# A transformer block and a linear attention block on one core: style preparation from VectorE to ScalarE, and the last two exponent rounds joined

## The chip, the cores and the metric
The kernel runs on one core of one Trainium2 chip. The metric is device time in microseconds of one launch, the median of several runs. One profiled execution stands beside them; its span, from the first to the last instruction, is what the views of the trace show.

## The reference
The input x holds 16 sequences of 128 tokens with 128 features, fp32. A conditioned transformer block is followed by a conditioned linear attention block:

```python
# block 1 (16 heads of 8 dimensions)
mod = c @ ada_w.T + ada_b                     # shift, scale, gate, twice
h = rmsnorm(x) * (1 + sc) + sh
q, k, v = split(h @ qkv_w.T)
q, k = rope(rmsnorm(q)), rope(rmsnorm(k))
attn = softmax(q @ k.T / sqrt(8))
x = x + g_msa * (attn @ v @ proj_w.T + proj_b)
h2 = rmsnorm(x) * (1 + sc2) + sh2
x = x + g_mlp * ((silu(h2 @ w1.T) * (h2 @ w3.T)) @ w2.T)
# block 2
xn = layer_norm(x) * norm_g + norm_b
q, k, v = xn @ Wq + bq, xn @ Wk + bk, xn @ Wv + bv
y = softmax_d(q) @ (softmax_n(k).T @ v)
scale, shift = split(silu(emb) @ emb_W + emb_b)
h = layer_norm(y, sn_g, sn_b) * (1 + scale) + shift
out = x + gate * (silu(h) @ out_W + out_b)
```

## The kernel before
The program is written by hand engine by engine; each engine has one instruction stream, and semaphores tie them together. A prologue loads and transposes the weights. Then the main loop runs over t = 0 to 17 (LAST_A = B + 2). Its pass t works on several sequences at once: scores of sequence t + 2, exponent products of sequence t, weighted values of t, their transposition to tokens and division for t - 1, the output projection of t - 2, and the front (norm, modulation, queries, keys, values) of t + 6. From t = 14 on the feed-forward of the first pairs of sequences (units) starts inside the loop: b_first, b_input and b_rest. After the loop blocks_tensor, blocks_vector, blocks_scalar and blocks_gpsimd finish the feed-forward and run the second block.

Attention scores are computed twice. First TensorE makes queries times keys for all four groups of heads, and VectorE takes each row's negated maximum (rowmax, L1604) and writes it into the padded queries, whose keys hold a one at that place. Then TensorE makes keys times queries again with the maximum subtracted in the product, and ScalarE takes the exponent straight from PSUM (exp, L1302). Heads have 8 dimensions, padded to 16, so one product uses 32 rows of the array: a row group. round_(t, r) (L1870) issues the scores of sequence t + 2 on two row groups (L1886) and the exponent products of sequence t on the other two (L1895), for r = 0 and 1. Scores go to banks 0 and 1 (S_BANK), exponent products to banks 2 and 3 (E_BANK), in both rounds, so round 1 waits until ScalarE has read round 0's banks (s_p) and VectorE the scores' (s_max). For t = 14 and 15 there is no sequence t + 2 left, and both rounds hold exponent products only.

weighted_values(t, r) (L1975) multiplies values by the exponents of round r; ScalarE's summed(t) (L1371) copies the result, TensorE's token_major(t) and projection(t - 1) follow in the next pass. ScalarE's order in a pass is: exp(t, 0), from t = 15 on the tanh of hidden column 0, from t = 14 on b_input (L566), queries_and_max (L1328), exp(t, 1), attended (L1363), from t = 15 on the tanh of hidden columns 1 and 2 (L575), summed(t), spread_of(t - 2), and at t = 10 outw (L1473).

hidden(t, p, c) on TensorE (L863, L864) makes column block c of the feed-forward's hidden layer; the banks are GU_BANK = (0, 1, 4). At t = 15 b_first makes block 0 after projection and token_major, and b_rest makes blocks 1 and 2 between weighted_values(15, 0) and weighted_values(15, 1).

The preparation of block 2's parameters is spread over the loop. style() (L1564) on VectorE, issued at the end of t = 8, makes csilu (the silu of the condition, two operations of 128x16), nbb (norm_b in all columns, 128x128) and lin (the three weights times norm_g, 128x384). prepare_biases(part) (L1834) on TensorE multiplies biases with the weights in three parts, at t = 10, 11 and 12; prepare_centred (L1853, product at L1855) follows at t = 13. biases() at t = 13 and centred() at t = 14 on VectorE copy the results. In the profile, lines of the page are those of the kernel printed below; L846 to L992 are TensorE's products of the feed-forward and of block 2.

Of the kernel before, what the change touches and what calls it, by code (L numbers as in the profile page):

```python
# [32 lines left out]
B, T, D = 16, 128, 128  # L33
# [13 lines left out]
NC = 4  # L47
# [65 lines left out]
def dit_then_linear_attention(nc, x, cond, pos, norm1_w, qkv_w, q_norm_w, k_norm_w, proj_w, proj_b,  # L113
# [3 lines left out]
    with ctx:  # L117
# [104 lines left out]
        def two(name, *shape):  # L222
# [45 lines left out]
        GU_BANK, F_BANK, X_BANK = (0, 1, 4), (2, 3), 7  # L268
# [139 lines left out]
        A_SQUARE, A_QKV, A_MID, A_SIN, A_ADA, A_W1, A_W3, A_TANH, A_GB, A_DONE, A_ROWS, A_SQUARES, A_OUTW = (  # L408
            1, 2, 3, 4, 5, 6, 7, 8, 9, 11, 12, 20, 21)
        V_COND, V_ADA1, V_MS, V_MOD, V_QKW, V_ANG, V_MSMID, V_MODR, V_MODS, V_LIN, V_BIAS, V_DONE = (  # L410
            2, 3, 5, 8, 9, 18, 20, 22, 24, 28, 34, 35)
# [24 lines left out]
        def scored(b, r, i):  # L436

            if b < EARLY:
                return ((s_s0, s_s1), (h_s0, h_s1))[r][i], b + 1
            return (s_s0, s_s1)[i], ROUNDS * b + r - 1  # L440

# [396 lines left out]
        def blocks_tensor(e, start=None):  # L838
# [14 lines left out]
            def hidden(t, p, c):  # L853
                u = t + 1
                if is_unit(u):
                    if c == 0:
                        e.wait_ge(b_hT, u + 1)
                        if at(u, 0):
                            e.wait_ge(s_max, NC * B)
                            e.wait_ge(s_kq, B)  # L860
                            e.wait_ge(pv_v, V_DONE)
                    wait(e, b_ff, FC * (u - 1) + c + 1)
# [48 lines left out]
            def c_step(t):  # L911
# [25 lines left out]
                if is_part(u):  # L937
                    hold_clock(t, 2 if t < C_UNITS + 3 else 4)
                    e.wait_ge(d_hs, u + 1)
                    if u == 0:  # L940
                        e.wait_ge(pv_a, A_OUTW)
# [309 lines left out]
        def _(a):  # L1251
# [44 lines left out]
            def exp(t, r, i):  # L1296
# [5 lines left out]
                q.activation(probs[2 * r + i][:, :, :, :].rearrange("p f a t -> p (f a t)"), bank[E_BANK[i]][:, :],  # L1302
# [144 lines left out]
            for t in range(LAST_A):  # L1447
# [23 lines left out]
                if t == B - 6:  # L1471
                    a.wait_ge(ld_rest, N_REST)
                    q.activation(outw[:, :], outw_n[:, :], ACT.Copy, scale=0.5).then_inc(pv_a, 1)  # L1473
            blocks_scalar(a, 2)
# [4 lines left out]
        def _(v):  # L1479
# [84 lines left out]
            def style():  # L1564

                v.wait_ge(pv_a, A_TANH)
                did(q.scalar_tensor_tensor(csilu[:, :], ctanh[:, :], 1.0, condT[:, :], ALU.add, ALU.mult))
                did(q.tensor_scalar(csilu[:, :], csilu[:, :], 0.5, None, ALU.mult))
                count(q.tensor_scalar(nbb[:, :], par[:, R_NB:R_NB + 1].to_broadcast([128, 128]), 1.0, None, ALU.mult))
                v.wait_ge(ld_rest, N_REST)  # L1570
                count(q.tensor_scalar(lin[:, :, :], lin_n[:, :, :], par[:, R_NG:R_NG + 1], None, ALU.mult))
                assert n == V_LIN

            def biases():
# [3 lines left out]
                did(q.tensor_tensor(embr[:, :, :], bank[W_BANK][:, 3 * D:3 * D + 2 * B].rearrange("p (c b) -> p c b", b=B),  # L1578
                                    par[:, R_EB:R_EB + 2].unsqueeze(2).to_broadcast([128, 2, B]), ALU.add))
# [501 lines left out]
```

## Time and profile before
| what | value |
|---|---|
| median of 3 runs | 207.35 us (207.1 to 209.03) |
| the profiled execution, its own time | 207.43 us |
| its span | 205.4 us |
| TensorE (PE) busy | 180.9 us, 88% of the span |
| VectorE (DVE) busy | 166.1 us, 81% |
| GpSimd (POOL) busy | 141.3 us, 69% |
| ScalarE (ACT) busy | 129.4 us, 63% |
| DMA | 8.30 MB, mean 40 GB/s |

Busy shares are means over the whole span; the stretch that the change touches is from 77 to 127 us, and a small edit near 36 us. PEld is TensorE's weight load, which overlaps its products. An fp32 product counts as two records of each kind, so the 8 products of a round of exponents show as 16 records. In a timeline "[0.35 <-PE bank L1895]" means that the engine had been idle for 0.35 us, and that the instruction named ended the wait.

### The profile page before, as it was taken

To read this page: it belongs to the slowest core of one execution; us is meant where nothing else is said; L and a number is where in the kernel's file an instruction comes from. 1 tells how busy PE (TensorE), PEld (TensorE's weight loads), DVE (VectorE), ACT (ScalarE), POOL (GpSimd) and SP (SyncE) were. 2 spreads that over 40 slices of the span, in tenths; PEclk is the share of its full clock that TensorE was granted. 3 is DMA by queue.
4 is the path that set the end of the run, shared out by engine and by line. 5 is a ranking of instruction groups with operands and counts; after the bars stand their busy time and mean duration, and the time that the engine had idled before them with its cause. 6 is when DMAs were issued, how large, how long until landed. Compare 5 with 4: busy or idle time off the path is not lost.

```text
span 205.4 us, 6100 instructions
## 1 busy us (share of the span) xinstructions
PE 180.9 (88%) x2039; PEld 142.3 (69%) x2039; DVE 166.1 (81%) x498; ACT 129.4 (63%) x377; POOL 141.3 (69%) x333
## 2 busy tenths in 40 slices
PE   2598887997999999799999998899998899999963
PEld 2345565786687777677676777799997677888642
DVE  6699898896989999997776534668889799999882
ACT  1367798776867777576546763454442468999741
POOL 8889798998989797958810682434542847668651
PEclk9999999999999999999999999999999999999999
DMA  5955006800000000000000000000000000010111
GB/s 93 289 137 207 0 10 254 359 6 0 3 3 2 5 5 0 3 0 5 3 3 0 5 0 3 0 0 5 2 0 2 0 3 0 0 30 28 51 51 51
DMA packets 10428, 8.30 MB, mean 40 GB/s; under 512 B 3106, under 2 KB 9887, under 8 KB 9887
## 3 DMA queue, kind: packets, MB, share of 16 engines
q1 hardware_dynamic: 7006, 7.25, 10.3%
q10 hardware_dynamic: 3392, 0.68, 1.7%
q8 instruction: 16, 0.26, 0.6%
q14 instruction: 14, 0.11, 0.2%
HBM read 6.86 MB, written 1.07 MB: 39 GB/s over the span
## 4 chain that ended last, share of the span: by engine, by line
PE 40%; DVE 17%; issue 8%; POOL 5%; ACT 4%; POOLq 0%; ACTq 0%; DVEq 0%
PE bank L1895 5%; DVE qkpad L1604 5%; PE bank L875 5%; PE bank L1886 5%; PE bank L863 5%; PE bank L864 4%; PE bank L1975 4%; ACT probs L1302 2%; PE bank L908 2%; POOL rstd L515 2%; PE bank L1907 1%; PE bank L1920 1%; PE bank L992 1%; PE bank L1949 1%; PE bank L972 1%
## 5 line engine op out<-in xcount | busy, mean ns | idle before, releaser
L1604 DVE TENSOR_REDUCE qkpad<-bank 128x4 f32<-128x512 f32 x64 | 41.0, 684 | 10.1 <-PE bank L1886 9.2
L1302 ACT ACTIVATE probs<-bank 128x512 f32<-128x512 f32 x64 | 34.7, 594 | 22.6 <-PE bank L1895 22.5
L1895 PE MATMUL bank<-qTm,kBD 32*128 32x128 f32 x512 | 37.1, 283 | 0.1
L1886 PE MATMUL bank<-kBD,qTs 32*128 32x256 f32 x224 | 32.0, 399 | 4.4 <-DVE qkpad L1604 3.4
L1895 PEld LDWEIGHTS bank<-qTm,kBD 32*128 32x128 f32 x512 | 31.0, 186 | 0.9 <-issue 0.6
L1886 PEld LDWEIGHTS bank<-kBD,qTs 32*128 32x128 f32 x224 | 19.7, 184 | 10.3 <-DVE qkpad L1604 6.3
L575 ACT ACTIVATE th<-bank 128x256 f32<-128x256 f32 x24 | 9.2, 384 | 19.4 <-PE bank L864 16.0
L1975 PE MATMUL bank<-probs,vpad 128*32 128x128 f32 x512 | 18.6, 277 | 2.0 <-ACT probs L1302 2.0
L1975 PEld LDWEIGHTS bank<-probs,vpad 128*32 128x32 f32 x512 | 12.6, 109 | 8.4 <-ACT probs L1302 7.3
L1130 POOL TENSOR_TENSOR partner<-qk,rope 128x96 f32<-128x96 f32 x32 | 14.4, 471 | 2.0 <-ACT qk L1344 2.0
L1949 PE MATMUL bank<-qkvT,hT 128*128 128x384 f32 x32 | 15.3, 571 | 0.5 <-ACT hT L1319 0.5
L1920 PE MATMUL bank<-ident,qkpad 128*128 128x128 f32 x96 | 14.2, 277 | 1.4 <-POOL qkpad L1192 1.1
L674 DVE SCALAR_TENSOR_TENSOR yg<-th,bank 128x256 f32<-128x256 f32 x24 | 10.1, 419 | 5.8 <-ACT th L575 5.8
L505 POOL TENSOR_TENSOR x<-fg,x 128x256 f32<-128x256 f32 x6 | 4.4, 730 | 14.9 <-DVE fg L691 14.9
L863 PE MATMUL bank<-hT,w1T 128*128 128x256 f32 x48 | 14.4, 382 | 0.0
L864 PE MATMUL bank<-hT,w3T 128*128 128x256 f32 x48 | 14.3, 379 | 0.0
L875 PE MATMUL bank<-w2T,ff 128*128 128x128 f32 x96 | 13.2, 275 | 0.0
L1920 PEld LDWEIGHTS bank<-ident,qkpad 128*128 128x128 f32 x96 | 10.8, 141 | 3.1 <-POOL qkpad L1192 1.7
L875 PEld LDWEIGHTS bank<-w2T,ff 128*128 128x128 f32 x96 | 12.4, 191 | 0.4
L515 POOL TENSOR_TENSOR rstd<-var,minus_half 128x2 f32<-128x2 f32 (+1 forms) x17 | 11.7, 687 | 1.4
L1141 POOL TENSOR_TENSOR rot<-qk,rope 128x256 f32<-128x256 f32 x16 | 11.7, 729 | 0.0
L1192 POOL TENSOR_TENSOR qkpad<-rot,ny 128x256 f32<-128x256 f32 x15 | 9.7, 647 | 2.2 <-DVE ny L1701 0.4
(253 smaller groups left out, 521.4 us busy)
## 6 DMA issues: line engine op xcount, KB each, us to landing
gate<-in_cond_dram SPq DMA_DIRECT2D x1, 1024.0 KB, 4.7
x<-gate_rows SPq DMA_DIRECT2D x1, 1024.0 KB, 4.3
y<-gate_rows SPq DMA_DIRECT2D x1, 1024.0 KB, 6.4
res<-gate_rows SPq DMA_DIRECT2D x1, 1024.0 KB, 9.8
out_dram<-res SPq DMA_DIRECT2D x7, 128.0 KB, 1.8
xin<-in_x_dram ACTq DMA_DIRECT2D x2, 256.0 KB, 5.4
xin<-in_x_dram SPq DMA_DIRECT2D x1, 512.0 KB, 5.7
ada_n<-in_L_cond_ada_w_dram SPq DMA_DIRECT2D x1, 256.0 KB, 6.2
```

Source lines behind the costliest of these rows:

```text
L515: q.tensor_tensor(rstd[:, rows], var[:, rows], minus_half[:, 0:rows.stop - rows.start], ALU.pow).then_inc(made, 1)
L863: q.matmul(bank[GU_BANK[c]][:, 0:UNIT * T], w1T[:, c * 128:c * 128 + 128], flat(hT2[1 - p]), start=True, stop=True)
L864: q.matmul(bank[GU_BANK[c]][:, UNIT * T:], w3T[:, c * 128:c * 128 + 128], flat(hT2[1 - p]), start=True, stop=True).then_inc(b_gu, 1)
L875: last = q.matmul(bank[F_BANK[j]][:, 0:D], ff[c][:, j * T:(j + 1) * T], w2T[:, c, :], start=c == 0, stop=c == FC - 1)
L1130: last = q.tensor_tensor(heads(partner[b % 2][:, :, :])[:, :, :, k::2], heads(qk[b % NQK][:, :, :])[:, :, :, 1 - k:ROPE:2], table(b, 1)[:, ...
L1302: q.activation(probs[2 * r + i][:, :, :, :].rearrange("p f a t -> p (f a t)"), bank[E_BANK[i]][:, :], ACT.Exp, scale=SCALE).then_inc(s_p, 1)
L1604: q.tensor_reduce(out_, score_bank(b, r, i)[:, :].rearrange("p (f a t) -> p f a t", f=2, a=2), X_AXIS, ALU.max, negate=True).then_inc(s_ma ...
L1886: last = q.matmul(bank[S_BANK[i]][:, f * 2 * T:(f + 1) * 2 * T], qTs[b % 2][rows, f, :], kBD[b % NKB][rows, f, :, :].rearrange("p a t -> p ...
L1895: last = q.matmul(bank[E_BANK[i]][:, (2 * f + k) * T:(2 * f + k + 1) * T], kBD[t % NKB][rows, f, k, :], qTm[t % 2][rows, f, :], start=True ...
L1920: last = q.transpose(dst[:, at_ + f * T:at_ + (f + 1) * T], qkpad[b % NKB][:, s, 8 * f:8 * f + 8, :].rearrange("p h d -> p (h d)"), ident[ ...
L1949: q.matmul(front_bank(b)[:, 128:512], hT[b % 2][:, :], qkvT[:, :], start=True, stop=True).then_inc(s_qkv, 1)
L1975: last = q.matmul(bank[O_BANK][32 * c:32 * c + 32, r * T:(r + 1) * T], vpad[b % NVP][:, col:col + VSTEP], probs[2 * r + i][:, f, k, :], st ...
```

## The change
style() keeps only the sum and product for csilu and is issued at t = 0; the factor 0.5 goes into embr. nbb and lin are made by ScalarE at the end of t = 10, behind outw. prepare_biases runs at t = 11, 12 and 13 and waits for ScalarE's two results (A_STYLE) in place of VectorE's. For t = 14 and 15 a new function exponents(t) issues all 16 exponent products of the sequence over four row groups, in four banks: those of r = 0 in banks 2 and 3, those of r = 1 in banks 0 and 1 (exp_bank); round_ isn't called there. It waits for all maxima (s_max). The hidden blocks go to banks 4, 0 and 1 in this order; block 0 of the first unit no longer waits for the maxima, blocks 1 and 2 wait for all exponents (s_p). weighted_values(t, 1) comes directly behind weighted_values(t, 0), ahead of b_rest at t = 15.

```diff
--- before.py
+++ after.py
@@ -265,7 +265,7 @@
 
         bank = [ctx.enter_context(nc.psum_tensor(f"bank{i}", [128, 512], F32)) for i in range(8)]
         S_BANK, E_BANK, T_BANK, P_BANK, O_BANK, W_BANK = (0, 1), (2, 3), 4, 5, 6, 7
-        GU_BANK, F_BANK, X_BANK = (0, 1, 4), (2, 3), 7
+        GU_BANK, F_BANK, X_BANK = (4, 0, 1), (2, 3), 7
         XC_BANK, QV_BANK, K_BANK, KT_BANK, CTX_BANK, QT_BANK, Y_BANK, XD_BANK, OUT_BANK = 7, 5, 6, 0, 1, 4, 2, 3, 0
 
 
@@ -405,10 +405,10 @@
         N_CONSTS = 10
         N_ROPE, N_ROPE_V = 8, 4
         P_COND, P_ADA1, P_MOD, P_QKV, P_ADA, P_MODS, P_PAR, P_W1, P_W3, P_W2, P_ROWS, P_BIAS, P_LIN = range(1, 14)
-        A_SQUARE, A_QKV, A_MID, A_SIN, A_ADA, A_W1, A_W3, A_TANH, A_GB, A_DONE, A_ROWS, A_SQUARES, A_OUTW = (
-            1, 2, 3, 4, 5, 6, 7, 8, 9, 11, 12, 20, 21)
-        V_COND, V_ADA1, V_MS, V_MOD, V_QKW, V_ANG, V_MSMID, V_MODR, V_MODS, V_LIN, V_BIAS, V_DONE = (
-            2, 3, 5, 8, 9, 18, 20, 22, 24, 28, 34, 35)
+        A_SQUARE, A_QKV, A_MID, A_SIN, A_ADA, A_W1, A_W3, A_TANH, A_GB, A_DONE, A_ROWS, A_SQUARES, A_STYLE = (
+            1, 2, 3, 4, 5, 6, 7, 8, 9, 11, 12, 20, 23)
+        V_COND, V_ADA1, V_MS, V_MOD, V_QKW, V_ANG, V_MSMID, V_MODR, V_MODS, V_CSILU, V_BIAS, V_DONE = (
+            2, 3, 5, 8, 9, 18, 20, 22, 24, 25, 31, 32)
 
         block = ctx.enter_context(nc.Block())
 
@@ -438,6 +438,10 @@
             if b < EARLY:
                 return ((s_s0, s_s1), (h_s0, h_s1))[r][i], b + 1
             return (s_s0, s_s1)[i], ROUNDS * b + r - 1
+
+        def exp_bank(b, r, i):
+
+            return bank[(S_BANK if r == 1 and b + 2 >= B else E_BANK)[i]]
 
         def front_bank(b):
 
@@ -856,9 +860,10 @@
                     if c == 0:
                         e.wait_ge(b_hT, u + 1)
                         if at(u, 0):
-                            e.wait_ge(s_max, NC * B)
                             e.wait_ge(s_kq, B)
                             e.wait_ge(pv_v, V_DONE)
+                    if c > 0 and at(u, 0):
+                        e.wait_ge(s_p, NC * B)
                     wait(e, b_ff, FC * (u - 1) + c + 1)
                     q.matmul(bank[GU_BANK[c]][:, 0:UNIT * T], w1T[:, c * 128:c * 128 + 128], flat(hT2[1 - p]), start=True, stop=True)
                     q.matmul(bank[GU_BANK[c]][:, UNIT * T:], w3T[:, c * 128:c * 128 + 128], flat(hT2[1 - p]), start=True,
@@ -938,7 +943,7 @@
                     hold_clock(t, 2 if t < C_UNITS + 3 else 4)
                     e.wait_ge(d_hs, u + 1)
                     if u == 0:
-                        e.wait_ge(pv_a, A_OUTW)
+                        e.wait_ge(pv_a, A_STYLE)
                     e.wait_ge(c_kxT, min(u + 4, C_UNITS))
                     for j in range(c_size(u)):
                         dst = bank[OUT_BANK][:, j * D:(j + 1) * D]
@@ -1299,7 +1304,7 @@
                     return
                 a.wait_ge((s_e0, s_e1)[i], ROUNDS * t + r + 1)
                 wait(a, s_o, ROUNDS * (t - 1) + r + 1)
-                q.activation(probs[2 * r + i][:, :, :, :].rearrange("p f a t -> p (f a t)"), bank[E_BANK[i]][:, :],
+                q.activation(probs[2 * r + i][:, :, :, :].rearrange("p f a t -> p (f a t)"), exp_bank(t, r, i)[:, :],
                              ACT.Exp, scale=SCALE).then_inc(s_p, 1)
 
             def spread_of(b):
@@ -1471,6 +1476,9 @@
                 if t == B - 6:
                     a.wait_ge(ld_rest, N_REST)
                     q.activation(outw[:, :], outw_n[:, :], ACT.Copy, scale=0.5).then_inc(pv_a, 1)
+                    q.activation(nbb[:, :], ident[:, :], ACT.Identity, bias=par[:, R_NB:R_NB + 1], scale=0.0).then_inc(pv_a, 1)
+                    q.activation(lin[:, :, :].rearrange("p c f -> p (c f)"), lin_n[:, :, :].rearrange("p c f -> p (c f)"), ACT.Identity,
+                                 scale=par[:, R_NG:R_NG + 1]).then_inc(pv_a, 1)
             blocks_scalar(a, 2)
 
 
@@ -1564,19 +1572,15 @@
             def style():
 
                 v.wait_ge(pv_a, A_TANH)
-                did(q.scalar_tensor_tensor(csilu[:, :], ctanh[:, :], 1.0, condT[:, :], ALU.add, ALU.mult))
-                did(q.tensor_scalar(csilu[:, :], csilu[:, :], 0.5, None, ALU.mult))
-                count(q.tensor_scalar(nbb[:, :], par[:, R_NB:R_NB + 1].to_broadcast([128, 128]), 1.0, None, ALU.mult))
-                v.wait_ge(ld_rest, N_REST)
-                count(q.tensor_scalar(lin[:, :, :], lin_n[:, :, :], par[:, R_NG:R_NG + 1], None, ALU.mult))
-                assert n == V_LIN
+                count(q.scalar_tensor_tensor(csilu[:, :], ctanh[:, :], 1.0, condT[:, :], ALU.add, ALU.mult))
+                assert n == V_CSILU
 
             def biases():
                 v.wait_ge(pt, P_BIAS)
                 count(q.tensor_copy(bias_qvo[:, :], bank[W_BANK][:, 0:3 * D]))
                 count(q.tensor_tensor(bias_k[:, :], bank[W_BANK][:, 3 * D + 2 * B:3 * D + 2 * B + 1], par[:, R_BK:R_BK + 1], ALU.add))
-                did(q.tensor_tensor(embr[:, :, :], bank[W_BANK][:, 3 * D:3 * D + 2 * B].rearrange("p (c b) -> p c b", b=B),
-                                    par[:, R_EB:R_EB + 2].unsqueeze(2).to_broadcast([128, 2, B]), ALU.add))
+                did(q.scalar_tensor_tensor(embr[:, :, :], bank[W_BANK][:, 3 * D:3 * D + 2 * B].rearrange("p (c b) -> p c b", b=B), 0.5,
+                                           par[:, R_EB:R_EB + 2].unsqueeze(2).to_broadcast([128, 2, B]), ALU.mult, ALU.add))
                 count(q.tensor_scalar(mods[:, :, A3], embr[:, 0, :], 1.0, par[:, R_SG:R_SG + 1], ALU.add, ALU.mult))
                 did(q.tensor_scalar(mods[:, :, S3], embr[:, 0, :], 1.0, par[:, R_SB:R_SB + 1], ALU.add, ALU.mult))
                 did(q.tensor_tensor(mods[:, :, S3], mods[:, :, S3], embr[:, 1, :], ALU.add))
@@ -1759,7 +1763,6 @@
                     b_rest(t - B)
                 if t == 0:
                     gates()
-                if t == B - 8:
                     style()
                 if t == B - 3:
                     biases()
@@ -1834,7 +1837,8 @@
             def prepare_biases(part):
 
                 if part == 0:
-                    e.wait_ge(pv_v, V_LIN)
+                    e.wait_ge(pv_a, A_STYLE)
+                    e.wait_ge(pv_v, V_CSILU)
                     e.wait_ge(s_v, B)
                     e.wait_ge(ld_rest, N_REST)
                     e.wait_ge(consts, 5)
@@ -1893,6 +1897,22 @@
                                 row = 32 * (2 * r + i)
                                 rows = slice(row, row + 32)
                                 last = q.matmul(bank[E_BANK[i]][:, (2 * f + k) * T:(2 * f + k + 1) * T], kBD[t % NKB][rows, f, k, :],
+                                                qTm[t % 2][rows, f, :], start=True, stop=True)
+                                if f == 1 and k == 1:
+                                    last.then_inc((s_e0, s_e1)[i], 1)
+
+            def exponents(t):
+
+                e.wait_ge(s_qTm, t + 1)
+                e.wait_ge(s_max, NC * B)
+                e.wait_ge(s_p, NC * t)
+                for f in range(2):
+                    for k in range(2):
+                        for r in range(2):
+                            for i in range(2):
+                                row = 32 * (2 * r + i)
+                                rows = slice(row, row + 32)
+                                last = q.matmul(exp_bank(t, r, i)[:, (2 * f + k) * T:(2 * f + k + 1) * T], kBD[t % NKB][rows, f, k, :],
                                                 qTm[t % 2][rows, f, :], start=True, stop=True)
                                 if f == 1 and k == 1:
                                     last.then_inc((s_e0, s_e1)[i], 1)
@@ -2020,7 +2040,10 @@
             modulation_rows()
             b_first, b_input, b_rest = blocks_tensor(e)
             for t in range(LAST_A):
-                round_(t, 0)
+                if t < B - 2:
+                    round_(t, 0)
+                elif t < B:
+                    exponents(t)
                 projection(t - 2)
                 token_major(t - 1)
                 if t == B - 1:
@@ -2033,20 +2056,21 @@
                 queries_and_max(t + 1)
                 queries_and_keys(t + 3)
                 input_turned(t + 6)
-                if B - 6 <= t < B - 3:
-                    prepare_biases(t - (B - 6))
+                if B - 5 <= t < B - 2:
+                    prepare_biases(t - (B - 5))
                 if t == B - 3:
                     prepare_centred()
                 if t == B - 2:
                     b_input(t - B, t % 2)
-                round_(t, 1)
+                if t < B - 2:
+                    round_(t, 1)
                 queries_keys_values(t + 6)
                 if t < B:
                     attended(t - 1)
                 weighted_values(t, 0)
+                weighted_values(t, 1)
                 if t == B - 1:
                     b_rest(t - B, t % 2)
-                weighted_values(t, 1)
                 if t >= B:
                     b_input(t - B, t % 2)
                     b_rest(t - B, t % 2)
```

## Rows read from the trace of the kernel before

**Rows 1.** The page, chain that ended last: shares of the span by engine.
```profile
PE 40%; DVE 17%; issue 8%; POOL 5%; ACT 4%; POOLq 0%; ACTq 0%; DVEq 0%
```
**Rows 2.** Busy time by stretch (from:to length, busy us (count) per engine, granted clock, DMA).
```profile
65.22:71.24 6.02, 5.63 (x98) 4.45 (x94) 5.92 (x15) 4.37 (x13) 4.93 (x15) 1.00 0.02 4
71.24:76.86 5.62, 5.62 (x98) 4.48 (x94) 4.97 (x13) 4.42 (x14) 5.36 (x12) 1.00 0.02 4
...
82.60:89.46 6.86, 5.64 (x99) 4.46 (x95) 6.78 (x17) 4.40 (x14) 4.98 (x10) 1.00 0.01 2
89.46:95.28 5.82, 5.41 (x97) 4.25 (x94) 5.63 (x14) 3.48 (x11) 4.50 (x14) 1.00 0.01 4
...
113.27:118.54 5.27, 4.84 (x77) 3.74 (x73) 2.52 (x11) 4.10 (x11) 3.90 (x7) 1.00 0.02 5
118.54:126.40 7.86, 7.31 (x88) 5.70 (x84) 3.03 (x10) 5.35 (x16) 5.56 (x12) 1.00 0.01 2
126.40:155.00 28.60, 28.07 (x178) 25.48 (x179) 22.07 (x75) 12.43 (x38) 12.13 (x22) 1.00 0.00 1
```
**Rows 3.** Timeline of VectorE, step 9 (start us, us, engine, line, operation, out<-in).
```profile
83.03 0.39 DVE L1567 SCALAR_TENSOR_TENSOR csilu<-ctanh,condT 128x16 f32<-128x16 f32 x1
83.46 0.65 DVE L1568 TENSOR_SCALAR csilu<-csilu 128x16 f32<-128x16 f32 x1
84.14 0.43 DVE L1569 TENSOR_SCALAR nbb<-par 128x128 f32<-128x128 f32 x1
84.50 0.64 DVE L1571 TENSOR_SCALAR lin<-lin_n,par 128x384 f32<-128x384 f32 x1
85.06 1.28 DVE L1604 TENSOR_REDUCE qkpad<-bank 128x4 f32<-128x512 f32 x2
```
**Rows 4.** Timeline of TensorE, step 9, its second round.
```profile
86.39 0.48 PE L1886 MATMUL bank<-kBD,qTs 32*128 32x256 f32 x2 [1.22 <-DVE qkpad L1604]
```
**Rows 5.** Timeline of VectorE after t = 0.
```profile
36.52 0.69 DVE L1604 TENSOR_REDUCE qkpad<-bank 128x4 f32<-128x512 f32 x1 [0.80 <-PE bank L1886]
```
**Rows 6.** Timeline of ScalarE, first exponent of step 11.
```profile
96.60 0.60 ACT L1302 ACTIVATE probs<-bank 128x512 f32<-128x512 f32 x1 [0.32 <-PE bank L1895]
```
**Rows 7.** Chain that ended last, steps 11 and 12 (start us, us, what).
```profile
97.09 0.66 PE bank L1920 x6
...
103.56 0.41 PE bank L1845 x2
...
104.75 0.32 PE bank L1886
```
**Rows 8.** Timeline of ScalarE, step 14.
```profile
115.60 0.81 ACT L566 ACTIVATE hT<-bank,mods 128x128 f32<-128x128 f32 x2
116.31 0.38 ACT L1328 ACTIVATE qTm<-bank 128x256 f32<-128x256 f32 x1
116.83 1.08 ACT L1302 ACTIVATE probs<-bank 128x512 f32<-128x512 f32 x2
```
**Rows 9.** Timeline of ScalarE, step 15.
```profile
122.55 1.08 ACT L1302 ACTIVATE probs<-bank 128x512 f32<-128x512 f32 x2 [0.22 <-PE bank L1895]
...
125.31 0.38 ACT L575 ACTIVATE th<-bank 128x256 f32<-128x256 f32 x1 [0.48 <-PE bank L864]
125.91 0.38 ACT L1371 ACTIVATE oT<-bank 128x256 f32<-128x256 f32 x1 [0.22 <-PE bank L1975]
```
**Rows 10.** Chain that ended last, step 15.
```profile
123.35 0.63 PE bank L863 x2
...
125.27 0.57 PE bank L1975 x16
```
**Rows 11.** Timeline of TensorE: early scores, weighted values, a round of exponents alone.
```profile
21.13 1.15 PE L1865 MATMUL bank<-kBD,qTs 32*128 32x256 f32 x16 [0.56 <-DVE qTs L1641]
...
75.85 1.08 PE L1975 MATMUL bank<-probs,vpad 128*32 128x128 f32 x32
...
113.27 1.16 PE L1895 MATMUL bank<-qTm,kBD 32*128 32x128 f32 x16
```

## The prediction
> **What bounds the kernel now.** I read the chain of work that ended last first, then the table of busy time by stretch, then the timelines of single engines. In the chain TensorE leads with 40% and VectorE follows with 17% [rows 1]. So neither is the bound everywhere, and each edit must be priced in its own step. I call step t the pass of the main loop that starts with TensorE's round_(t, 0); the table's stretches are steps 6, 7, 9, 10, 14, 15 and what follows up to 155 us [rows 2]. The granted clock is 1.00, the upper level of 2.4 GHz, in all of them, so no clock effect enters.
>
> In steps 6 and 7 TensorE is busy 5.63 and 5.62 us, but the steps last 6.02 and 5.62. Even steps, where VectorE also seeds the square roots of the head norms, are set by VectorE (5.92 of 6.02); odd steps by TensorE. Step 9 is odd and has TensorE's usual 5.64 busy, yet it lasts 6.86, with VectorE busy 6.78 [rows 2]. In steps 14 and 15 TensorE is busy 4.84 of 5.27 and 7.31 of 7.86; these hold the rounds that the change joins. ScalarE's exponents stand between TensorE's products there.
>
> **The style work leaves VectorE (step 9).** style() is issued at the end of t = 8 and runs in step 9: 0.39 + 0.65 + 0.43 + 0.64 = 2.11 us, and the row maxima behind it start at 85.06 [rows 3]. TensorE's second round waits for them 1.22 us [rows 4]. With the block gone step 9 becomes like step 7: 6.86 - 5.62 = 1.24 us won. The two ways of pricing it agree within 0.02. It can't be 2.11, as the products behind the maxima end only later.
> The one operation that stays on VectorE (csilu, 0.39) now runs at t = 0, where VectorE stands idle 0.80 us before its next maxima [rows 5]. Its input is ready before the loop, so it costs nothing; without that cover it would cost 0.39. Folding the factor 0.5 into embr changes one small operation for another of about its size, off the path.
>
> **ScalarE takes nbb and lin (end of t = 10).** Before shows no such activation. nbb (128x128) I price at the 0.40 of one of the two 128x128 modulations (0.81 for both) [rows 8]. lin (128x384) lies between the 128x256 copy, 0.38 [rows 9], and the 128x512 exponent, 0.60 [rows 6]; it is nearer the upper in elements and has a pointer scale besides, so 0.55. Together at most 1.0, some 0.75 after overlap of neighbours. ScalarE had 0.32 idle there before its exponents at 96.60 [rows 6], so these start about 0.4 late, and end 1.1 later at 98.1. TensorE's transposes end at 97.75, and the bias product that now follows them (0.41) fills it till 98.2 [rows 7]. Cost: 0 to 0.1, I take 0.05. If that cover went, it would be the 0.4.
> "ScalarE: Activation LUTs" of the Trainium skill ("Rules for kernel authors") speaks against this move: simple multiplies and adds belong on VectorE, which is faster per element. VectorE's 0.64 and 0.43 [rows 3] against the two prices above don't bear it out; by the rule ScalarE's start would slip past TensorE's cover, and the sum would be up to 0.4 higher.
>
> **The bias products move one step later on TensorE.** Part 2 lasts 104.75 - 103.56 = 1.19, and its first product, which streams about as much as part 0 and part 1 do each, 0.41 [rows 7]. Part 0 leaves step 10; in step 11 it takes the place of part 1, no change; part 1 takes the place of part 2 in step 12, and part 2 enters step 13.
> - Step 10: TensorE is ready 0.41 sooner; that is the most that can be won. At worst the step becomes like step 6, 6.02 against its 5.82 [rows 2]: +0.2. VectorE is busy 5.63 of 5.82 there and lets little through, so I take half the gain, -0.2.
> - Step 12: 1.19 - 0.41 = 0.78 won; the chain runs through part 2 without a break, and nothing else ends later than part 1 would.
> - Step 13: the chain also runs through the product before the second round, so all of 1.19 is added. VectorE reads these products at the end of the step, later than they then come.
> Steps 10 to 13 and ScalarE's 0.05: -0.2 - 0.78 + 1.19 + 0.05 = +0.26.
>
> **The joined rounds (steps 14, 15).** A round of exponents alone has 16 records on two row groups and takes 1.16. The early scores have 16 records on all four row groups, of twice the columns, thus the array work of a joined round, in 1.15; the weighted values put 32 records through four column groups in 1.08 [rows 11]. Before has no case of 32 records over four row groups. Lower bound 1.1: the groups run side by side and issue is no limit. Upper end 2.3: two rounds in a row. Two rows of the three stand near the lower one, so I take 1.2, thus 0.05 late per step.
> "TensorE: Matmul & The Clock Gate" of the Trainium skill ("Back-to-back issue gap") has 81 ns per sustained pair of load and product at 128 columns. By it a joined round takes 2.6 and the sum is about 2.8 higher; the weighted values' 34 ns a pair disagree for tiled products.
> What a joined round frees is a second round of 1.1 on TensorE. What takes its place is ScalarE's fixed order:
> - Step 14: exponents, two modulations, the copy qTm, exponents. qTm starts at 116.31 and, 0.38 long with neighbours overlapping by 0.1, would let exponents start at 116.6; before they started at 116.83 [rows 8]. Won 0.24, less 0.05. All of TensorE's other time is given back waiting for the last exponent.
> - Step 15: exponents started at 122.55 and ended at 123.63, after 0.22 idle; with the 0.1 by which neighbours overlap they come 0.3 sooner, 123.33 [rows 9]. But before, TensorE did the hidden products of columns 1 and 2 meanwhile (123.35 to 125.27, 1.92 [rows 10]), and the last weighted values (0.57) after. These products now write the banks that the last exponents read, and stand behind the weighted values. So: exponents end 123.33; weighted values till 124.0; hidden products till 125.9; tanh of column 2 starts 125.95 (before 125.31); the copy of the sums follows at 126.25 (before 125.91). It is 0.34 later, and TensorE's next projection with it. With 0.05 for the round: +0.39.
> The wait for s_max in exponents(14) costs nothing, since the maxima of the last sequence end before the weighted values of step 13 do. Behind the new wait for s_p on TensorE stand the two hidden products, and behind them tanh, the gate on VectorE and the copy of the sums: that is the 0.39. The bank permutation changes no duration. No DMA is issued, moved or passed by any edit. From 126.4 to 155 TensorE is busy 28.07 of 28.60 us [rows 2] with work that doesn't change, so whatever shift stands at 126.4 reaches the end.
> Steps 14 and 15: -0.19 + 0.39 = +0.20.
>
> **Sum.** -1.24 + 0.26 + 0.20 = -0.78 us. The profiled execution took 207.43 (span 205.4), 0.08 above the median 207.35. 207.4 - 0.8 = 206.6.
>
> **Rivals.**
> A. VectorE is late again in step 10 and gives back part of step 9: the even pattern of 6.02 [rows 2] in place of my 5.62 costs 0.4, 207.0. For it: VectorE is busy 5.63 of 5.82. Against: VectorE carries the same seeds in step 10 before the change too, and the step still takes 5.82. Chance 0.15.
> B. TensorE alone binds steps 14 and 15, and both removed rounds count in full: 2 x 1.16 in place of +0.20, 204.1. Against it: before the last exponents ScalarE is idle 0.22 only [rows 9], so it can't come 1.16 sooner. Chance 0.06.
> C, on the other side. The 32 pairs don't overlap beyond what two row groups show: 1.16 / 16 = 72 ns each, 2.3 us for a joined round. Then the first exponent of steps 14 and 15 starts 1.1 later, 2.2 in all less the 0.1 counted: 208.7, slower than before. It decides from where a joined round takes about 1.55 us (0.4 more in each step). Against it: the early scores and the weighted values [rows 11]. Chance 0.08. The figure of the Trainium skill's clock gate page, above, would make it slower still.
> D. The hidden products behind the last weighted values delay the whole gate: all 1.92 shows instead of 0.34, 208.1 at most. Against: the copy of the sums waits only for tanh of column 2. Chance 0.06.
> My forecast has the other 0.65.
>
> **Numbers.** 1% of 207.35 is 2.07, about what a measurement of this kernel can tell from no change. The range runs from the forecast's own lower edge (step 10 at -0.4, joined rounds at 1.1, ScalarE's activations free: 206.3, and 0.7 for step lengths that differ by 0.4 within one pattern: 205.6) to 207.9, near D's full price; it leaves out B and C, and a little beside, 0.2. Faster by over 1% needs 205.28 or less: B and a rest, 0.07. Slower by over 1% needs 209.42: C with more, 0.03. Within 1%: 0.90.
>
> **What would show it.** Right: step 9 at 5.6 and no wait for maxima in it; step 12 0.8 shorter and step 13 1.2 longer; 32 records of exponents in about 1.2; TensorE waiting for exponents over 1 us in steps 14 and 15; projection of sequence 14 starting 8.2 after step 15's start, not 7.86. Wrong: joined rounds over 1.5 us (C), step 15 under 7.5 us (B), step 10 at 6 us (A).

## The result and the profile after

The changed kernel takes 206.48 us, the median of 16 runs (206.18 to 207.55); the kernel before, beside it, 207.37 (207.01 to 209.03). The ratio is 0.995, with a 95% interval of 0.9933 to 0.9966. That is 0.9 us less; the forecast was 206.6, 0.8 less.

The profiled execution of after took 207.28 us with a span of 205.6, longer than the span of before (205.4). It is not a typical one: late in it TensorE's granted clock fell to the lower level, 1.2 GHz (0.74 on average in the last row here, 0.50 from 199.65 to 202.50), which costs 1.1 us, as the last section works out. So the steps are compared one by one, in stretches where the granted clock is 1.00. The table of busy time by stretch of after, for steps 9 to 15, for what follows up to the same work as at 155 us in before, and for the end:

```profile
core 0: us, PE busy (x) PEld busy (x) DVE busy (x) ACT busy (x) POOL busy (x), PEclk, DMA share, GB/s
82.53:88.15 5.62, 5.62 (x99) 4.48 (x95) 4.94 (x13) 4.42 (x14) 4.87 (x10) 1.00 0.01 3
88.15:93.66 5.51, 5.04 (x95) 4.00 (x91) 5.41 (x14) 3.46 (x10) 4.35 (x13) 1.00 0.02 4
93.66:99.54 5.88, 5.48 (x97) 4.28 (x93) 4.83 (x11) 4.17 (x12) 5.37 (x12) 1.00 0.02 3
99.54:105.37 5.83, 5.37 (x98) 4.16 (x94) 4.37 (x11) 3.29 (x9) 2.34 (x5) 1.00 0.00 0
105.37:112.24 6.87, 6.46 (x101) 4.80 (x97) 3.62 (x9) 3.29 (x9) 0.00 (x0) 1.00 0.01 2
112.24:117.27 5.03, 3.70 (x77) 2.79 (x74) 2.14 (x11) 3.98 (x11) 3.75 (x6) 1.00 0.02 5
117.27:125.46 8.19, 6.15 (x88) 4.72 (x84) 2.74 (x9) 5.13 (x16) 5.69 (x13) 1.00 0.00 0
...
125.46:154.06 28.60, 28.07 (x178) 25.48 (x179) 22.34 (x76) 12.43 (x38) 12.13 (x22) 1.00 0.01 2
199.00:205.60 6.60, 3.27 (x15) 2.25 (x15) 1.39 (x5) 0.77 (x2) 1.24 (x3) 0.74 0.13 40
```

The same table of before has steps 9, 10, 14 and 15 in [rows 2]; steps 11, 12 and 13 are:

```profile
95.28:101.10 5.82, 5.36 (x97) 4.15 (x94) 4.49 (x10) 3.49 (x10) 5.44 (x11) 1.00 0.02 3
101.10:107.67 6.57, 6.16 (x103) 5.02 (x99) 4.27 (x10) 3.29 (x9) 2.12 (x5) 1.00 0.01 2
107.67:113.27 5.60, 5.19 (x93) 3.81 (x89) 3.62 (x9) 3.29 (x9) 0.00 (x0) 1.00 0.00 0
```

Step lengths in us, measured and forecast:

| | step 9 | 10 | 11 | 12 | 13 | 14 | 15 | sum |
|---|---|---|---|---|---|---|---|---|
| before | 6.86 | 5.82 | 5.82 | 6.57 | 5.60 | 5.27 | 7.86 | 43.80 |
| after | 5.62 | 5.51 | 5.88 | 5.83 | 6.87 | 5.03 | 8.19 | 42.93 |
| difference | -1.24 | -0.31 | +0.06 | -0.74 | +1.27 | -0.24 | +0.33 | -0.87 |
| forecast | -1.24 | -0.2 | +0.05 | -0.78 | +1.19 | -0.19 | +0.39 | -0.78 |

The 28.60 us behind step 15 are 28.60 in both, to the hundredth, with 28.07 of TensorE's work. What stands at step 15's end does reach the end. It comes at 125.46 in place of 126.40, 0.94 sooner: 0.87 by these seven steps, and 0.07 that was already won at the start of step 9 (82.53 against 82.60).

In steps 14 and 15 TensorE has 1.14 and 1.16 us less to do than before (3.70 against 4.84, 6.15 against 7.31), a whole round each. The steps change by -0.24 and +0.33.

TensorE's timeline of after in steps 14 and 15 (start us, us, engine, line, operation, out<-in; in brackets the idle time before and what ended it):

```profile
112.24 1.17 PE L1915 MATMUL bank<-qTm,kBD 32*128 32x128 f32 x32
...
115.81 0.30 PE L2005 MATMUL bank<-ident,o 128*128 128x128 f32 x1 [1.32 <-ACT qTm L1333]
...
117.27 1.17 PE L1915 MATMUL bank<-qTm,kBD 32*128 32x128 f32 x32
...
122.09 0.65 PE L1995 MATMUL bank<-probs,vpad 128*32 128x128 f32 x16 [1.25 <-ACT probs L1307]
...
124.07 0.59 PE L869 MATMUL bank<-hT,w3T 128*128 128x256 f32 x2
125.46 0.46 PE L1927 MATMUL bank<-projT,oT 128*128 128x128 f32 x2 [0.80 <-issue]
```

The 32 records of a joined round take 1.17 us, 37 ns each; 16 records on two row groups take 1.16 [rows 11]. "TensorE: Matmul & The Clock Gate" of the Trainium skill ("Back-to-back issue gap") has 81 ns a pair; this trace does not agree for 32-row tiles. What was won shows as idle time: 1.32 before the transposes of step 14, 1.25 before the last weighted values.

ScalarE's timeline of after, step 15, shows why nothing comes of it there:

```profile
120.95 1.09 ACT L1307 ACTIVATE probs<-bank 128x512 f32<-128x512 f32 x2
...
123.84 0.39 ACT L579 ACTIVATE th<-bank 128x256 f32<-128x256 f32 x1 [1.63 <-PE bank L869]
124.70 0.38 ACT L579 ACTIVATE th<-bank 128x256 f32<-128x256 f32 x1 [0.48 <-PE bank L869]
124.98 0.38 ACT L1376 ACTIVATE oT<-bank 128x256 f32<-128x256 f32 x1
```

The copy of the sums (L1376) needs only the weighted values, which end at 122.7. It stands behind two tanh in ScalarE's fixed order, and these wait for the hidden products. TensorE's projection at 125.46 comes right behind the copy, which ends at 125.36; that it waits for the copy is tested below (sum_first), as the profile names only "issue" there.

### The profile page after: what moved, and what is told of

It is laid out like the page before. It is cut to its first block, busy times and chain, and to the rows that moved or that the text cites. A ratio compares the mean times of both kernels' runs of the same rounds, so it can differ in the third digit from the quotient of the medians.

```text
span 205.6 us, 6098 instructions
## 1 busy us (share of the span) xinstructions
PE 180.2 (88%) x2039; PEld 141.5 (69%) x2039; DVE 164.2 (80%) x495; ACT 129.8 (63%) x379; POOL 141.0 (69%) x333
## 3 DMA queue, kind: packets, MB, share of 16 engines
HBM read 6.86 MB, written 1.07 MB: 39 GB/s over the span
## 4 chain that ended last, share of the span: by engine, by line
PE 45%; DVE 14%; issue 8%; ACT 6%; POOL 3%; POOLq 0%; ACTq 0%; DVEq 0%
PE bank L1890 5%; PE bank L880 5%; PE bank L868 5%; PE bank L869 4%; PE bank L1995 4%; DVE qkpad L1608 4%; PE bank L1899 4%; PE bank L997 2%; ACT probs L1307 2%; PE bank L913 2%; PE bank L1940 2%; PE bank L1927 2%; PE bank L1969 2%; PE bank L1915 1%; PE bank L977 1%
## 5 line engine op out<-in xcount | busy, mean ns | idle before, releaser
L1899 PE MATMUL bank<-qTm,kBD 32*128 32x128 f32 x448 | 32.5, 283 | 0.0
L1899 PEld LDWEIGHTS bank<-qTm,kBD 32*128 32x128 f32 x448 | 27.1, 186 | 0.0
```

Source lines behind the costliest of these rows:

```text
L1899: last = q.matmul(bank[E_BANK[i]][:, (2 * f + k) * T:(2 * f + k + 1) * T], kBD[t % NKB][rows, f, k, :], qTm[t % 2][rows, f, :], start=True ...
```

## The experiments

All ratios are to the kernel before, measured beside each; its median was 207.11 for the first four experiments and 207.23 for the other four.

**One part each.** only_style is after with rounds, banks and order of before:

```
-        GU_BANK, F_BANK, X_BANK = (4, 0, 1), (2, 3), 7
+        GU_BANK, F_BANK, X_BANK = (0, 1, 4), (2, 3), 7
...
-                if t < B - 2:
-                    round_(t, 0)
-                elif t < B:
-                    exponents(t)
+                round_(t, 0)
...
-                if t < B - 2:
-                    round_(t, 1)
+                round_(t, 1)
...
                 weighted_values(t, 0)
-                weighted_values(t, 1)
                 if t == B - 1:
                     b_rest(t - B, t % 2)
+                weighted_values(t, 1)
```

> The style preparation and the bias products are moved as in the change, the exponent rounds and the hidden banks stay as before. Theory (the gain is the gap that the style work left in step 9, and the joined rounds cancel): steps 9 to 13 sum to -1.24 - 0.31 + 0.06 - 0.75 + 1.28 = -0.96 against before by the profile after, plus 0.1 measured ahead of step 8, so 206.4, ratio 0.995. Rival (the joined rounds bring part of the gain): this kernel gets at most half of the 0.89, 206.9.

Measured: 206.16 us, ratio 0.9958 (0.9936 to 0.9979). That is 0.95 us less. The rival, at most half of the change's 0.89, needs a ratio of 0.9979 or more, which is the very edge of the interval; the next experiment decides. only_rounds is the opposite, before with the joined rounds and all that goes with them:

> The joined exponent rounds, the hidden banks and the order of the weighted values alone, on the kernel before. Theory: step 14 is 0.24 shorter and step 15 0.33 longer, 207.4 to 207.5, ratio 1.0005. Rival (each removed round of 1.1 us on TensorE counts): 205.2, ratio 0.989.

Measured: 207.10 us, ratio 1.0004 (0.9985 to 1.0022). TensorE's timeline of only_rounds, the joined rounds and the projection of step 16:

```profile
113.41 1.17 PE L1916 MATMUL bank<-qTm,kBD 32*128 32x128 f32 x32
...
118.44 1.17 PE L1916 MATMUL bank<-qTm,kBD 32*128 32x128 f32 x32
...
126.63 0.46 PE L1928 MATMUL bank<-projT,oT 128*128 128x128 f32 x2 [0.80 <-issue]
```

118.44 - 113.41 = 5.03 and 126.63 - 118.44 = 8.19 are the step lengths of after. So the rounds come to -0.24 + 0.33 = +0.09 us, and a gain of two whole rounds (2.3 us, a ratio of 0.989) lies outside the interval. All that the change wins, it wins by the style work.

**Only the first round joined.** join14 joins for the sequence before the last and leaves the last as before, its hidden banks, waits and order of products too (the excerpt shows the rounds alone):

```
-                if t < B - 2:
-                    round_(t, 0)
-                elif t < B:
-                    exponents(t)
+                if t == B - 2:
+                    exponents(t)
+                else:
+                    round_(t, 0)
...
-                if t < B - 2:
+                if t != B - 2:
                     round_(t, 1)
```

> The changed kernel, but only sequence 14 has the joined round; sequence 15 has its two rounds, its banks and the hidden products between the weighted values, as before. Theory (the join costs in step 15 and gains in step 14): 0.33 less than the changed kernel, 206.15, ratio 0.994, and step 15 lasts 7.86 again instead of 8.19. Rival (the two joins are worth the same, or both nothing): as the changed kernel, 206.5.

Measured: 206.05 us, ratio 0.9941 (0.9921 to 0.9962). In its trace the projection stands at 125.36, with 0.55 idle before it in place of 0.80, 12.88 after step 14's start; in after that is 5.03 + 8.19 = 13.22. So -0.34 us, the price of the second joined round together with the order of products that it brings, found from the other side. The ratios alone, 0.9941 and 0.995, could not show it.

**The copy of the sums first.** sum_first lets ScalarE issue it ahead of the tanh, once:

```
+                if t == B - 1:
+                    summed(t)
                 if t >= B - 1:
                     b_rest(t - B)
                 if t >= B:
                     attended(t - 1)
-                summed(t)
+                if t != B - 1:
+                    summed(t)
```

> The changed kernel with one move on ScalarE at t = 15: the copy of the sums (summed) comes ahead of the tanh of hidden columns 1 and 2 instead of behind them. Theory (in step 15 TensorE's wait of 0.80 us before the projection of sequence 14 is only ScalarE's order): TensorE goes on from the hidden products to the projection at once, step 15 lasts 7.4 instead of 8.19, total 205.7, ratio 0.992. Rival (the wait is needed by something else, such as the gate products on VectorE, and comes back within step 16): 206.5 as the changed kernel, with the step after 0.8 longer.

Measured: 205.19 us, ratio 0.9912 (0.9883 to 0.9941). ScalarE's timeline of sum_first, the copy, which now waits only for the weighted values:

```profile
122.67 0.39 ACT L1376 ACTIVATE oT<-bank 128x256 f32<-128x256 f32 x1 [0.60 <-PE bank L1998]
```

Its TensorE timeline, the last hidden product and the projection, with no idle time between:

```profile
123.94 0.59 PE L869 MATMUL bank<-hT,w3T 128*128 128x256 f32 x2
124.37 0.39 PE L1930 MATMUL bank<-projT,oT 128*128 128x128 f32 x2
```

And its table by stretch, step 15 and the 32 matmul records behind it:

```profile
117.14:124.37 7.23, 5.99 (x88) 4.87 (x85) 1.81 (x7) 4.75 (x13) 5.66 (x13) 1.00 0.00 0
124.37:129.76 5.39, 4.86 (x32) 4.18 (x30) 4.38 (x15) 2.74 (x10) 1.59 (x3) 1.00 0.02 3
```

The 0.80 before the projection is gone, step 15 lasts 7.23 in place of 8.19, and the next stretch doesn't give it back (5.39; from 125.46 to 130.93, 5.47, in after). So ScalarE's order had held 0.96 us of step 15. Against before's 7.86 that is 0.63 won in step 15. How much of it is the joined round's, and how much would come from the new order of the products and of the copy with two separate rounds, is not shown: no run has that order with two rounds. The order alone could at most fill TensorE's wait before the projection, 0.55 without the join (join14).

**Place or engine.** late_dve gives nbb and lin back to VectorE, but at the end of t = 10; csilu stays at t = 0:

```
                 if t == B - 6:
                     a.wait_ge(ld_rest, N_REST)
                     q.activation(outw[:, :], outw_n[:, :], ACT.Copy, scale=0.5).then_inc(pv_a, 1)
-                    q.activation(nbb[:, :], ident[:, :], ...).then_inc(pv_a, 1)
-                    q.activation(lin[:, :, :]..., lin_n[:, :, :]..., ...).then_inc(pv_a, 1)
...
                     style()
+                if t == B - 6:
+                    style_rest()
```

> The changed kernel with nbb and lin back on VectorE, but at the end of t = 10 (csilu stays at t = 0) instead of on ScalarE there. Theory (the gain came from the place, since VectorE has an idle gap of over 1 us before the maxima of step 11 that holds 0.43 + 0.64 us): as the changed kernel, ratio 0.995, step 11 still 5.8 to 5.9. Rival (VectorE can't take this work anywhere in the loop, the engine matters): the maxima of step 11 come about 1 us late, as they did in step 9, ratio 0.999, step 11 at 6.8.

Measured: 206.11 us, ratio 0.9944 (0.9922 to 0.9966). VectorE's timeline of late_dve at that place:

```profile
93.71 0.21 DVE L1578 TENSOR_SCALAR nbb<-par 128x128 f32<-128x128 f32 x1
93.84 0.78 DVE L1579 TENSOR_SCALAR lin<-lin_n,par 128x384 f32<-128x384 f32 x1
```

ScalarE's timeline of after at the same place:

```profile
94.57 0.39 ACT L1479 ACTIVATE nbb<-ident,par 128x128 f32<-128x128 f32 x1
94.86 0.60 ACT L1480 ACTIVATE lin<-lin_n,par 128x384 f32<-128x384 f32 x1
```

VectorE takes 0.21 + 0.78, ScalarE 0.39 + 0.60: the same sum. late_dve's step 11, from TensorE's scores at 93.58 to those at 99.40, lasts 5.82, as in before; in after it lasts 5.88. So for these two operations the engine is worth 0.06, and the gain of step 9 didn't need ScalarE. VectorE's own work is 4.94 of 5.62 in step 9 of after, which leaves 0.68 for style's 2.11; in step 11 it is 4.83 of 5.88, which leaves 1.05 for these 0.99. The other 1.04 of the 2.11 were the two operations for csilu, one of which is gone and one at t = 0 in late_dve too; what nbb and lin alone would cost in step 9 no run shows. "ScalarE: Activation LUTs" of the Trainium skill ("Rules for kernel authors") puts multiplies and adds on VectorE, with a factor that it gives for bf16. These operations are fp32, and the traces show no clear winner: at 384 columns ScalarE took 0.60 and VectorE 0.78 here and 0.64 in before, at 128 columns ScalarE 0.39 and VectorE 0.21 here and 0.43 in before [rows 3].

**The centring product.** In after it runs in step 13, where TensorE is busy 6.46 of 6.87; in step 14 TensorE waits 1.32. centre14 moves it there:

```
-                if t == B - 3:
-                    prepare_centred()
                 if t == B - 2:
                     b_input(t - B, t % 2)
+                    prepare_centred()
```

> The changed kernel with the centring product (0.65 us on TensorE) moved from before the second round of step 13 to step 14 behind the transposes of the feed-forward's input, where TensorE waits 1.32 us for ScalarE. Theory (bias and centring products ahead of the second round of step 13 stand in full on the path, and step 14 is bound by ScalarE): 0.65 less than the changed kernel, 205.6 to 205.8, ratio 0.992; step 13 at 6.2, step 14 still 5.03. Rival (step 13 is bound by the maxima, or step 14 by TensorE): as the changed kernel, ratio 0.995.

Measured: 205.50 us, ratio 0.9924 (0.9897 to 0.9951). TensorE's timeline of centre14, from the projection in step 13:

```profile
106.59 0.49 PE L1927 MATMUL bank<-projT,oT 128*128 128x128 f32 x2
...
111.62 1.18 PE L1915 MATMUL bank<-qTm,kBD 32*128 32x128 f32 x32
...
113.70 0.81 PE L1859 MATMUL bank<-lin,centre 128*128 128x384 f32 x2
115.19 0.30 PE L2005 MATMUL bank<-ident,o 128*128 128x128 f32 x1 [0.67 <-ACT qTm L1333]
```

Projection to joined round is 5.03 (after: 112.24 - 106.47 = 5.77), so -0.74. Step 14 still lasts 5.03: the product of 0.81 took 0.65 of the wait, which falls from 1.32 to 0.67.

**Everything together.** combo has the edits of sum_first, centre14 and late_dve. It also moves parts 0 and 1 of the bias products, and the four products of the condition, from before the second round to between the two halves of the weighted values, where TensorE waits about 0.4 us for exponents. Part 2's other products stay before the second round of step 13:

```
-                if B - 5 <= t < B - 2:
-                    prepare_biases(t - (B - 5))
                 if t == B - 3:
-                    prepare_centred()
+                    prepare_biases(2)
...
                 weighted_values(t, 0)
+                if t == B - 5:
+                    prepare_biases(0)
+                if t == B - 4:
+                    prepare_biases(1)
+                if t == B - 3:
+                    prepare_biases(3)
                 weighted_values(t, 1)
```

> A try at a better version: the changed kernel with the copy of the sums ahead of the tanh at t = 15, the centring product in step 14, nbb and lin on VectorE at the end of t = 10, parts 0 and 1 of the bias products between the two weighted values of steps 11 and 12 (where TensorE waits about 0.4 for the exponent), and part 2 split, its products with the condition between the weighted values of step 13. By the theory: -0.95 (sums) - 0.65 (centring) - 0.4 (condition's products) - 0.2 (parts 0 and 1; the maxima bind there) against the changed kernel, 204.3, ratio 0.985. Rival (the gaps overlap each other and only the first two add): 204.9, ratio 0.988.

Measured: 203.81 us, ratio 0.984 (0.9813 to 0.9867), 3.4 us less than before and the best version found. TensorE's timeline of combo, the projections of steps 11 and 12:

```profile
94.87 0.49 PE L1936 MATMUL bank<-projT,oT 128*128 128x128 f32 x2
...
100.56 0.49 PE L1936 MATMUL bank<-projT,oT 128*128 128x128 f32 x2
```

The same timeline, the condition's products between the weighted values in step 13, the joined rounds, and the projection behind them:

```profile
109.77 0.62 PE L1861 MATMUL bank<-csilu,emb_n 128*128 128x16 f32 x4
110.32 0.65 PE L2004 MATMUL bank<-probs,vpad 128*32 128x128 f32 x16
110.89 1.17 PE L1924 MATMUL bank<-qTm,kBD 32*128 32x128 f32 x32
...
115.92 1.17 PE L1924 MATMUL bank<-qTm,kBD 32*128 32x128 f32 x32
...
123.14 0.38 PE L1936 MATMUL bank<-projT,oT 128*128 128x128 f32 x2
```

From the projection of step 11 to that of step 16 combo takes 123.14 - 94.87 = 28.27, after 125.46 - 94.77 = 30.69: -2.42. The parts: step 15 -0.96, centring product -0.74, the two periods between the projections of steps 11, 12 and 13 (5.69 each against 5.88 and 5.82) -0.32, of which 0.06 is nbb and lin on VectorE, and step 13 again, 110.89 - 106.25 = 4.64 against centre14's 5.03, -0.39. They add to -2.41. With after's own gain of about 0.9 to 1.0 that is the 3.4 measured. The parts add up, so they don't disturb each other: each fills or removes another wait.

**The clock at the end.** TensorE's timeline of after near the end:

```profile
196.65 0.33 PE L913 MATMUL bank<-ident,xs 128*128 128x128 f32 x1 [0.90 <-DVE xs L821]
196.82 0.60 PE L850 MATMUL bank<-warm 128*128 128x256 bf16 x4
...
199.46 0.39 PE L913 MATMUL bank<-ident,xs 128*128 128x128 f32 x1 [1.18 <-DVE xs L821]
199.65 1.06 PE L850 MATMUL bank<-warm 128*128 128x256 bf16 x4
```

The same four filler products take 0.60 at 196.8 and 1.06 at 199.65, behind a wait of 1.18. warm8 is after with 8 filler products in place of 2 ahead of the last two parts' transposes:

```
-                    hold_clock(t, 2)
+                    hold_clock(t, 2 if t < C_UNITS + 3 else 8)
```

> The changed kernel with 8 instead of 2 of the filler products before the transposes of the last two parts (t = 12 and 13 of the last loop), where TensorE waits 0.90 and 1.18 us for VectorE. In the profile of the changed kernel the granted clock fell to 1.2 GHz at 199.5 us and the last 6 us took 1.1 us longer. Theory (idle time of TensorE just ahead lets the clock fall in some executions): the median stays at 0.995, but no or few executions have a mean clock of 0.992 and 1.1 us more. Rival (the fall has another cause): about a quarter of them still have it.

Measured: 206.08 us, ratio 0.9946 (0.9925 to 0.9967). The wait before the last transpose is 0.53 and the fillers behind it take 0.60. None of its six runs is the 1 us longer; but of the kernel before only 7 of the 35 runs measured beside the experiments lie 0.8 us or more above their median, and at one in five, six runs without one come about one time in four. So it is inconclusive. What sets the fall off stays open. It occurs in the kernel before too: six of the 25 runs measured beside the first experiments have a span of 206.1 to 206.5 in place of about 205.2, at a mean clock of 0.992. The step lengths above come from stretches at 1.00 and don't hold it; the medians and their intervals do, as a part of the noise.

## Why the prediction was right

- **Step 9, -1.24.** Exact. The row maxima start at 83.69 in place of 85.06 [rows 3], and behind an idle 0.65:

```profile
83.69 1.29 DVE L1608 TENSOR_REDUCE qkpad<-bank 128x4 f32<-128x512 f32 x2 [0.65 <-PE bank L1890]
```

  TensorE's wait of 1.22 for them [rows 4] is gone. Removed were 2.11 us of work and 1.24 us of time. VectorE's busy time falls by 1.84 (6.78 to 4.94; neighbours had overlapped), and the maxima now wait 0.65 for TensorE's products: 1.84 - 0.65 = 1.19, near the 1.24. Pricing the gap, not the work, was the step that carried the forecast.
- **csilu at t = 0, 0.** It takes 0.54, not the 0.39 used, and the idle time before the next maxima falls from 0.80 [rows 5] to 0.36. Covered, and only_style loses nothing by it.

```profile
35.55 0.54 DVE L1575 SCALAR_TENSOR_TENSOR csilu<-ctanh,condT 128x16 f32<-128x16 f32 x1
36.46 0.69 DVE L1608 TENSOR_REDUCE qkpad<-bank 128x4 f32<-128x512 f32 x1 [0.36 <-PE bank L1890]
```

- **ScalarE's nbb and lin.** Estimated 0.40 and 0.55, measured 0.39 and 0.60. The exponents behind them start 1.71 after the step's start (95.37 - 93.66) in place of 1.32 (96.60 - 95.28): 0.39 late, for 0.4. TensorE's cover held: step 11 +0.06 for +0.05, and late_dve, without these two on ScalarE, is back at 5.82.
- **Step 10, -0.31 for -0.2.** Part 0 was taken too small: 0.41 was read from part 2's first product, and called the most that can be won. In before part 0 holds the second round back by 92.29 - 91.76 = 0.53. TensorE's timeline of before:

```profile
91.76 0.60 PE L1841 MATMUL bank<-lin_n,nbb 128*128 128x256 f32 x2
92.29 0.48 PE L1886 MATMUL bank<-kBD,qTs 32*128 32x256 f32 x2
```

  VectorE's and TensorE's timelines of after, the maxima and the second round:

```profile
89.31 1.29 DVE L1608 TENSOR_REDUCE qkpad<-bank 128x4 f32<-128x512 f32 x2
...
90.70 0.48 PE L1890 MATMUL bank<-kBD,qTs 32*128 32x256 f32 x2
```

  The round comes 2.55 after the step's start (88.15) in place of 2.83, so 0.28 sooner, and right behind the maxima, which end at 90.60. So the reason for taking half was right: VectorE lets about half of the 0.53 through. With the step at 5.51 rival A (6.02) falls.
- **Steps 12 and 13, -0.74 and +1.27** for -0.78 and +1.19. The move of part 2 cost its full length, as the chain said. TensorE's busy time in step 13 rises from 5.19 to 6.46, which is the whole 1.27; in step 12 it falls from 6.16 to 5.37. Part 2 itself was not taken too small: from its first product (107.32) to the centring product (108.43) it takes 1.11. The rest is its neighbours, which follow each other less closely: from the transposes to it 0.31 in place of 0.22, and the centring product holds the second round back by 0.82 in place of 0.74. combo shows what the forecast didn't ask: the place before the second round is the dear one. The condition's products cost 0.46 there (centre14 against combo) and 0.07 between the weighted values, part 0 0.28 there (late_dve against combo) and 0.15 between them.
- **The joined round, 1.17 for 1.2.** Of the three neighbours [rows 11], the early scores (1.15) were the right one. Rival C needed 1.55 and falls.
- **Step 14, -0.24 for -0.19, and step 15, +0.33 for +0.39.** The -0.19 holds 0.05 for a slower round, which only cost 0.01. The projection of the last but one sequence was forecast 8.2 after step 15's start, and stands at 8.19. Rival B (step 15 under 7.5) and rival D (all 1.92 shown) fall. The objection to B, that ScalarE can't come 1.16 sooner, holds even in combo: its step 14 lasts 5.03 as well.
- **What the working left out.** The copy of the sums was followed as a victim (0.34 later), but not asked whether it has to stand where it does. Its own input ends at 122.7; 0.96 us lay in that order, about as much as the whole change brought. With the copy moved ahead, steps 14 and 15 come to -0.24 + 0.33 - 0.96 = -0.87 us against before, by the joined rounds and the new order together; the order's own share in step 15 is not shown.
- **The lower edge of the range.** Its terms (step 10 at -0.4, joined rounds at 1.1 in place of 1.2, ScalarE free) take 0.2 + 0.2 + 0.05 from 206.6, which is 206.15 and not 206.3. The measured 206.48 lies above both.

## What to carry to other kernels

When work leaves an engine, price the wait that the next engine has for it, and when work enters, look for the place where that engine already waits: here leaving step 9 was worth 1.24 us, and the choice between the two engines at the new place 0.06. When an edit frees a busy engine and the step hardly moves, read the in-order queue of the engine that it now waits for, and ask of each instruction ahead of the awaited one whether the awaited one needs it. With 16 runs of each kernel a gain of 0.5% stands clear of no change (0.9933 to 0.9966), but the small differences between its parts do not; the steps of the trace at one clock show them, and the span of a single profiled execution can show the opposite sign.

## What the hardware showed that I had not expected

- 32 records of 32-row products on four row groups take as long (1.17) as 16 on two (1.16), so a record costs half.
- Near the end TensorE's granted clock can fall to the lower level, 1.2 GHz, behind a wait of 1.18 us. The same waits, 0.90 and 1.18, with the same products between them, were followed by the upper level, 2.4 GHz, in the profiled execution of before (granted clock 1.00 from 200.41 to the end), whose timeline of TensorE has there:

```profile
200.41 0.33 PE L908 MATMUL bank<-ident,xs 128*128 128x128 f32 x1 [1.18 <-DVE xs L817]
200.58 0.60 PE L846 MATMUL bank<-warm 128*128 128x256 bf16 x4
```

  From the transpose behind the second wait to the end of the span it is 205.6 - 199.46 = 6.1 us in after and 205.4 - 200.41 = 5.0 in before: 1.1 us, more than the change brings.
- The same operation on VectorE has different durations in different places: csilu's 128x16 took 0.39 in step 9 [rows 3] and 0.54 at t = 0, nbb's 128x128 took 0.43 in step 9 [rows 3] and 0.21 in late_dve. So the price of a small one, read from another place, can be off by a third to a half.
